# Reordering the next block's norm matmuls, q/k pieces and values around the projection and LayerNorm 2 of an adaLN transformer layer

## The reference, cut to what matters

```
def _phi(x, omega):                       # features of q and of k
    proj = einsum('bhtd,dm->bhtm', x, omega)
    norm_sq_half = 0.5 * sum(x * x, axis=-1, keepdims=True)
    return exp(proj - norm_sq_half) / sqrt(m)

h = layernorm(x) * (1 + ca) + sa
q, k, v = split(h @ W_attn + b_attn)      # q and k scaled
S, Z = cumsum(phi_k * v), cumsum(phi_k)   # over time
y = (phi_q . S) / (phi_q . Z + EPS)
x = x + ga * (y @ W_proj + b_proj)
h = layernorm(x) * (1 + cb) + sb
logits = h @ Wg + bg; w = softmax gates of the best 2 of 4 experts
out = sum_e w_e * (relu(h @ Wi + (h @ A_e) @ B_e) @ Wo)
x = x + gb * out
```

## Time and profile before

| | us |
|---|---|
| median of 3 runs | 823.14 |
| the runs | 819.2, 823.56, 823.14 |
| the profiled execution | 823.59 |
| its span | 821.3 |
| TensorE busy | 764.2 (93% of the span) |
| VectorE busy | 541.1 (66%) |
| ScalarE busy | 412.3 (50%) |
| GpSimd busy | 62.2 (8%) |

### The profile page before, as it was taken

One profiled execution on the slowest core, in us unless ns is written; L12 is line 12 of the kernel. 1 busy time (PEld: TensorE's weight loads), 2 busy tenths in 40 slices (PEclk: granted clock), 3 DMA queues, 4 the chain that ended last, 5 costly groups with the idle time before them and its releaser, 6 DMA issues.

```text
span 821.3 us, 16965 instructions
## 1 busy us (share of the span) xinstructions
PE 764.2 (93%) x6138; PEld 605.1 (74%) x6138; DVE 541.1 (66%) x1276; ACT 412.3 (50%) x764; POOL 62.2 (8%) x72
## 2 busy tenths in 40 slices
PE   3989999999999999999999999999999999998696
PEld 3767768876698767977688776977679776986466
DVE  5347676676767766776776766776767767666456
ACT  2475445554456554654366444555455644563222
POOL 1261000010002000010000100010000100010000
PEclk9979999999999999999999999999999999999689
DMA  7850172203702073201812055010732028010000
GB/s 260 226 139 1 43 195 54 77 0 106 182 0 77 0 204 84 77 0 52 209 26 77 0 134 153 16 61 2 208 77 77 0 79 206 3 52 2 0 1 26
DMA packets 42867, 65.35 MB, mean 80 GB/s; under 512 B 5064, under 2 KB 19168, under 8 KB 42720
## 3 DMA queue, kind: packets, MB, share of 16 engines
q1 hardware_dynamic: 42848, 65.09, 29.4%
HBM read 39.91 MB, written 25.17 MB: 79 GB/s over the span
## 4 chain that ended last, share of the span: by engine, by line
PE 85%; DVE 8%; ACT 3%; issue 2%; SPq 1%; DMA 1%; DVEq 0%; POOL 0%; ACTq 0%
PE pa L512 11%; PE prod L527 7%; PE ring L491 6%; PE ring L375 6%; PE pa L375 5%; PE ring L376 4%; PE ring L377 4%; PE pa L377 4%; PE pa L376 4%; PE prod L546 4%; PE pa L619 4%; PE ring L496 3%; PE ring L642 2%; PE prod L512 2%; PE ring L695 2%; PE prod L536 2%
## 5 line engine op out<-in xcount | busy, mean ns | idle before, releaser
L512 PE MATMUL pa<-phq,phkT 128*128 128x128 f32 x896 | 115.4, 276 | 0.0
L512 PEld LDWEIGHTS pa<-phq,phkT 128*128 128x128 f32 x896 | 108.3, 192 | 2.4 <-issue 1.6
L835 ACT ACTIVATE phq<-ring 128x512 f32<-128x512 f32 x96 | 59.0, 615 | 91.3 <-PE ring L491 90.3
L1076 DVE TENSOR_TENSOR am_phk<-pa,const 128x512 f32<-128x512 f32 x112 | 74.3, 686 | 33.0 <-PE pa L512 33.0
L1229 DVE SCALAR_TENSOR_TENSOR am_phk<-ring,am_phk 128x512 f32<-128x512 f32 x64 | 44.3, 691 | 53.2 <-PE ring L695 53.2
L375 PE MATMUL pa<-wo_r,qk_r 128*128 128x256 f32 x256 | 72.1, 282 | 0.6 <-DVE qk_l L1234 0.6
L897 ACT ACTIVATE qk_r<-phq 128x512 fp32r<-128x512 f32 x64 | 40.5, 632 | 63.7 <-DVE phq L1238 63.7
L377 PE MATMUL pa<-wo_l,qk_r 128*128 128x256 f32 x256 | 72.2, 282 | 0.0
L376 PE MATMUL pa<-wo_r,qk_l 128*128 128x256 f32 x256 | 71.8, 281 | 0.0
L527 PE MATMUL prod<-am_phk,v_ones 128*32 128x256 f32 x1024 | 61.9, 382 | 4.7 <-DVE tg L1107 4.7
L375 PE MATMUL ring<-h_r,wi_r 128*128 128x512 f32 x128 | 57.9, 452 | 4.2 <-DVE am_phk L1229 3.6
(11 more groups left out here) (204 smaller groups left out, 1578.0 us busy)
## 6 DMA issues: line engine op xcount, KB each, us to landing
xq<-qk_parts SPq DMA_DIRECT2D x48, 512.0 KB
qk_parts<-qk_r SPq DMA_DIRECT2D x32, 256.0 KB, 3.3
qk_parts<-qk_l SPq DMA_DIRECT2D x32, 256.0 KB, 3.6
tok<-in_L_attn_x SPq DMA_DIRECT2D x8, 512.0 KB, 4.7
xr<-in_L_attn_x SPq DMA_DIRECT2D x8, 512.0 KB, 4.0
out_x<-tg SPq DMA_DIRECT2D x16, 256.0 KB, 2.3
norm_parts<-norm_r SPq DMA_DIRECT2D x16, 128.0 KB, 3.2
norm_parts<-norm_l SPq DMA_DIRECT2D x16, 128.0 KB, 5.2
```

The costliest lines, as they stand in the source:

```text
L512: mm = pe.matmul(score_bank(q, a)[:, tt], phkT[:, q % 2, a, tt], phq[:, q // 2 % 2, 2 * (q % 2) + a, tt], start=True, stop=True)
L835: act.activation(dst, src, ACT.Exp).then_inc(exp_done.sem, 1)
L1076: dve.tensor_tensor(am[:, 2 * (q % 2) + a, :].rearrange("p (c t) -> p c t", c=NT), score_bank(q, a)[:].rearrange("p (c t) -> p c t", c=NT) ...
```

## The change

On TensorE the first norms of the next block move from ahead of y's transposition to behind it and ahead of the projection, and go to another bank (pb[0] in the place of pa[0]); the second half of q/k piece 3 moves behind the projection; the second norms move behind the transpositions of LayerNorm 2's tokens; the values follow the last q/k matmul. The waits go with them: the values wait for the first norms' split, the projection no longer does, and `ffn_head` waits for the split of the last q/k piece and of the first norms. On ScalarE q/k piece 2 is copied before y, the first norms behind y, the second norms behind h_r. On VectorE y is divided ahead of `split_qk(n + 1, 1)`, `split_qk(n + 1, 2)` stands ahead of `split_norm(n + 1, 0)`, and `split_norm(n + 1, 1)` behind the values. SyncE's program is as it was.

```diff
--- before.py
+++ after.py
@@ -206,7 +206,7 @@
         prod = ctx.enter_context(nc.psum_tensor("prod", [P, NT, 2, P], F32))
         pb = [prod[:, 2 * b:2 * b + 2].rearrange("p c k m -> p (c k m)") for b in range(2)]
         qk_bank = [pa[0], pa[1], ring[2], ring[3]]
-        norm_bank = [pa[0], ring[0]]
+        norm_bank = [pb[0], ring[0]]
         wo_bank, low_bank, lora_bank = [pa[0], pa[1], ring[0], ring[1]], ring[2], [ring[3], pa[0]]
         lead_bank = [pb[0], pb[1], pa[1], ring[0]]
         z_bank = [ring[3], ring[1], ring[0], ring[2]]
@@ -422,14 +422,13 @@
             def norms(n, half):
 
                 wait(pe, sq_ready, n, 2 * half + 2)
-                if half == 0:
-                    wait(pe, qk_split, n, 1)
                 for j in (2 * half, 2 * half + 1):
                     mm = pe.matmul(norm_bank[half][j * VA:(j + 1) * VA, :], headsum, qk_sq[:, j, :],
                                    start=True, stop=True)
                 mm.then_inc(norm_mm.sem, 1)
 
             def values(n):
+                wait(pe, norm_split, n, 1)
                 for t in range(NT):
                     dst = pb[t // 2][:, t % 2 * C:(t % 2 + 1) * C]
                     tt = slice(t * P, (t + 1) * P)
@@ -609,7 +608,6 @@
                 pe.wait_ge(wp_done.sem, B)
                 if front_next:
                     wait(pe, qk_split, n + 1, 2)
-                    wait(pe, norm_split, n + 1, 1)
                 row = n // BLOCKS_PER_ROW
                 for t in range(NT):
                     dst = pa[t // 2][:, t % 2 * C:(t % 2 + 1) * C]
@@ -631,12 +629,17 @@
 
             def ffn_head(n, front_next):
 
+                if front_next:
+                    wait(pe, qk_split, n + 1, 4)
+                    wait(pe, norm_split, n + 1, 1)
                 for t in range(NT):
                     wait(pe, h2n_ready[t // 2], n, t % 2 + 1)
                     for k, dst in enumerate((ring[3], ring[1])):
                         mm = pe.transpose(dst[:, t * P:(t + 1) * P], tok[:, t, k * P:(k + 1) * P], ident)
                         if t == NT - 1:
                             mm.then_inc(h2_ps.sem, 1)
+                if front_next:
+                    norms(n + 1, 1)
                 for k in range(KT):
                     wait(pe, h2_full[k], n, 1)
                     mm = pe.matmul(ring[2][:], low_t[:, k, :], h_f[:, k, :], start=k == 0, stop=k == KT - 1)
@@ -740,13 +743,12 @@
             def after_attend(n, front_next):
                 if front_next:
                     qk(n + 1, 3, [0])
+                y_transpose(n)
+                if front_next:
                     norms(n + 1, 0)
-                y_transpose(n)
+                projection(n, front_next)
                 if front_next:
                     qk(n + 1, 3, [1])
-                projection(n, front_next)
-                if front_next:
-                    norms(n + 1, 1)
                     values(n + 1)
                 ffn_head(n, front_next)
                 masks(n)
@@ -868,6 +870,8 @@
                 for k in range(KT):
                     wait(act, h2_full[k], n, 1)
                     act.activation(h_r[:, k, :], h_f[:, k, :], ACT.Copy).then_inc(h2_r.sem, 1)
+                if front_next:
+                    front_norm(n + 1, 1)
                 wait(act, lg_ps, n, 1)
                 act.activation(lg, ring[2][:], ACT.Copy).then_inc(lg_done.sem, 1)
                 act.activation(low.bitcast(F32R), ring[2][0:LROWS, :], ACT.Copy).then_inc(low_high.sem, 1)
@@ -913,12 +917,11 @@
                 if front_next:
                     front_qk(n + 1, 0)
                     front_qk(n + 1, 1)
+                    front_qk(n + 1, 2)
+                y_copy(n)
+                if front_next:
                     front_norm(n + 1, 0)
-                y_copy(n)
-                if front_next:
-                    front_qk(n + 1, 2)
                     front_qk(n + 1, 3)
-                    front_norm(n + 1, 1)
                 ffn(n, front_next)
 
             with act.Fori(0, NB - 1) as i:
@@ -1130,11 +1133,11 @@
                     elif front_next:
                         split_qk(n + 1, 0)
                     add_reads(n, gr)
-                    if front_next and not more:
-                        split_qk(n + 1, 1)
                     if gr == GROUPS - 2:
                         causal_scores(n, q + 1, 1)
                     divide(n, gr)
+                    if front_next and not more:
+                        split_qk(n + 1, 1)
                     if gr < GROUPS - 2:
                         causal_scores(n, q + 1, 1)
                     if front_next and gr == 0:
@@ -1283,20 +1286,19 @@
 
             def after_attend(n, front_next):
                 if front_next:
+                    split_qk(n + 1, 2)
                     split_norm(n + 1, 0)
-                    split_qk(n + 1, 2)
                 residual(n)
                 if front_next:
                     split_qk(n + 1, 3)
                 normalize_apply(n, xr, ln2_pool, h2n_ready[0])
-                if front_next:
-                    split_norm(n + 1, 1)
                 h2_copy(n)
                 if front_next:
                     values(n + 1, [0])
                 split_h(n, h2_r, 1, h2_parts)
                 if front_next:
                     values(n + 1, [1])
+                    split_norm(n + 1, 1)
                 ffn_rest(n, front_next)
 
             with dve.Fori(0, NB - 1) as i:
```

More of the change, by code:

```diff
@@ L742, in after_attend @@
                     qk(n + 1, 3, [0])
-                    norms(n + 1, 0)
                 y_transpose(n)
                 if front_next:
-                    qk(n + 1, 3, [1])
+                    norms(n + 1, 0)
                 projection(n, front_next)
                 if front_next:
-                    norms(n + 1, 1)
+                    qk(n + 1, 3, [1])
                     values(n + 1)
@@ L915, in after_attend @@
                     front_qk(n + 1, 1)
-                    front_norm(n + 1, 0)
+                    front_qk(n + 1, 2)
                 y_copy(n)
                 if front_next:
-                    front_qk(n + 1, 2)
+                    front_norm(n + 1, 0)
                     front_qk(n + 1, 3)
-                    front_norm(n + 1, 1)
                 ffn(n, front_next)
```

## The result

The changed kernel takes 816.52 us against 822.49 for the kernel before (medians of 7 executions each, side by side): ratio 0.995, 95% interval 0.9931 to 0.997. A second comparison of the same two programs gave 817.68 (12 executions) against 822.38 (23), ratio 0.995, interval 0.9932 to 0.9968. These ratios are not the quotients of the medians (816.52 / 822.49 = 0.993); they agree with those of the means, 817.59 / 821.86 and 817.84 / 821.94, which lie 4.3 and 4.1 us apart. Forecast were 818.9 us within 815.5 to 823.5, and 0.41 for a gain over 0.5%: the gain is clear of the noise, but both intervals hold 0.995, so whether it is over 0.5% stays open.

What follows compares the result with a forecast made beforehand. TensorE, through one dependency chain from y's last division to the low-rank matmuls, was taken to bound the kernel. 0.60 us a block over seven blocks gives 4.2 us: 823.14 - 4.2 = 818.9 us, range 815.5 to 823.5.

Steps and rivals of the forecast that it cites:

- Part 1, division: On VectorE, dividing y ahead of the second q/k split gains nothing: taken at 0, bound 0.08 us.
- Part 2, first norms: On TensorE, first norms behind y's transposition: the projection starts 0.55 to 0.65 us sooner in each block.
- Part 3, the way from the projection to the low-rank matmuls: Second norms behind the h transposition: the 9.92 us from projection to low-rank matmuls stay, at worst 0.1 us more.
- Nothing in the last block: In the last block, where none of the moved steps run, the change gains nothing.
- The DMA queue: On SyncE, moves into xq start 1.2 us later; second norms' store keeps 1.3 us before VectorE masks: cost 0.
- Rival (b): Second norms' store lands after VectorE wants to mask: slower, 838.5 us or about 828; chance 0.12.
- (a): y's transposition released more slowly, or second norms gate low-rank matmuls: about 0.3 us a block lost, 821.0 us; chance 0.13.
- (c): TensorE's clock falls with new gaps in each block, projection slow in seven blocks: 834.6 us; chance 0.02.
- (d): TensorE gets back both holes fully, at projection and low-rank matmuls: 1.0 us a block, 816.1 us; chance 0.05.

Runs made afterwards that it cites:

- The late store: Store of the second norms issued behind the second moves into xq instead of ahead of them, against the changed kernel: 889.02 us.

## Why the prediction was right, and where it was not

The direction and the range held, and so did the mechanism of the seven blocks. That the median lies as far down as it does is luck: it came with something that I had priced at zero.

*Part 1, division: 0.* Right, and shown alone.

*Part 2, first norms: 0.55 to 0.65 us at the projection.* Right: 2.63 - 2.06 = 0.57. Two details were off, both to the late side. ScalarE's copies begin 0.69 us after the transposition starts (0.63 assumed), and TensorE leaves the transpositions for the column-tiled norms after 1.02 us, not 0.84: the 0.1 us that I had allowed for the change of shape was 0.18. The two paths run side by side, so the errors do not add. The copies end at 291.27 + 1.08 = 292.35 and with the 0.20 of before would allow 292.55; TensorE comes free at 292.58. They are level within 0.03 us, and no run shows which of them sets the projection. That the first norms carry the gain is shown by moving them back.

*Part 3, the way from the projection to the low-rank matmuls: 9.92 us, at worst 0.1 more.* It is 302.61 - 292.58 = 10.03. Up to the h transposition it is unchanged (7.72 us in both), so the added waiting of TensorE in front of it (0.47 us) was indeed no cost. Then the second norms hold the low-rank matmuls by 0.11 us, for TensorE needs 1.32 us from L638 to L426 where I had 1.2, probably by the same change of shape. This is the term that the sum had too large: I had allowed for this delay "at worst" and taken it at nothing. 0.60 a block was taken, 0.49 measured (3.42 / 7), inside the stated 0.45 to 0.65. That the second norms fill a hole is true, and their place is worth 0.05 us a block.

*Nothing in the last block.* This step failed. The moved steps do not run there, but its time varies by 3.5 us, together with TensorE's clock, and the profiled execution of before had the longer form. Half of the span's difference between the two profiles comes from there. The seven blocks alone would give 822.49 - 3.4 = 819.1 us; the measured 816.52 has 2.5 us more, because the median of one kernel fell in its lower group and that of the other in its upper. The means, 4.3 and 4.1 us apart, hold less of this. The row was in front of me (5.95 us for a projection of 3.71 us) and I used it for a rival only.

*The DMA queue.* The first moves start 3.71 us after the first norms by my reckoning, hence at 296.4 for a block with y at 291.82, that is 4.6 us after y. They start 4.8 us after y:

```profile
295.31 1.52 SPq L339 DMA_DIRECT2D xq<-qk_parts  x3
...
306.35 0.60 SPq L335 DMA_DIRECT2D norm_parts<-norm_l  x1
```

The store issued at 306.35 lands 3.7 us later, at 310.05, and VectorE masks at 311.53: a margin of 1.5 us where I had 1.3. Rival (b) did not happen. The late store bears out its price, one us a block for each us beyond, and shows that the clock would probably have added to it.

*The rivals.* (a), part of the gain lost, happened in small: 0.1 us a block and not 0.3. (c), a clock that falls inside the blocks, did not happen: 1.00 from 80 to 759 us, with gaps of 0.31 and 0.47 us in each block. The Trainium skill (TensorE: Matmul & The Clock Gate, "HAM oscillation") says that waits between groups of matmuls can make the clock fall again and again; the last block of the kernel before (0.50 after waits of up to 1.17 us) and the late store (0.50 after one of 8.37 us) agree with it, and these gaps set nothing off. (d), both holes filled, is refuted by the changed kernel itself, which has no idle at L617 and L645 and gains 0.49 us a block, not 1.0: new waits opened ahead of the two transpositions. The experiment with the first norms back says the same of the second hole alone: filled, no gain.

## What to carry to other kernels

Follow the one chain of dependencies through a stretch and ask of every engine what it does ahead of each link: work that stands in front of a ready link costs the time by which it holds that link up (here 0.57 us a block for norms of 0.99), and work that only fills a hole behind it is worth next to nothing (0.05). Then look for the part of a link's input that is ready long before the rest; half of a transposition moved into the gap was worth 0.42 us a block, nearly as much as the whole reordering. When two profiles differ by more than the stage that was changed, compare them stage by stage before the difference is put down to the edit.

## What the runs showed of the hardware

Around y's last division TensorE idles in the last block by turns for 0.44 to 1.17 us, and the clock may or may not fall behind that. In the two profiled executions of the kernel before it fell to 0.50 (the 1.2 GHz level) at about 764 us, ahead of the projection. In those of the changed kernel, with the same waits, it was 1.00 there and fell first at about 770 us, after a wait of 3.80 us. So these waits alone do not settle it, and what else does is not known. The same program gives times 3 to 4 us apart. Cutting the wait of 1.01 us in that block to 0.58 went with a clock of 1.00 through the projection in the profile, and with mean clocks of 0.986 to 0.992 in all ten executions, where the kernel before goes down to 0.982. TensorE takes 0.18 us more from eight transpositions to column-tiled matmuls than from the same eight to plain matmuls (1.02 against 0.84 us).
